# Recurrent scan with a transformer tile beside it: the output projection's halves, their filler and the widening change places

## Chip, cores and metric

One core of a Trainium2 chip. The metric is the device time of one execution in microseconds, lower is better. TensorE can be granted one of two clocks, 1.2 or 2.4 GHz.

## What is computed

Input x is (4, 16, 16, 64): four images of 256 positions with 64 channels, float32. Three layers follow, each added to what it gets:

```
x = x + deformable_conv(group_norm(x))         # 3x3, bilinear samples
t = tokens(x)                                  # (4, 256, 64)
t = t + attention_block(layer_norm(t))         # 8 heads of 32
t = t + scan(layer_norm(t))                    # 256 steps in order
```

The attention block, with y its projected output:

```
y  = o @ w_out.T + b_out
x1 = layernorm(y + x)
ff = (gelu(y @ w1.T) * (y @ wv.T)) @ w2.T
return layernorm(ff + x1)
```

The scan, one step per token and all four images at once (the forget gate is computed by the reference, but enters nothing):

```
i, o = sigmoid(xi_t + h @ V_i), sigmoid(xo_t + h @ V_o)
g = tanh(xg_t + h @ V_c)
c_new = h * c + i * g
h_new = o * tanh(c_new)
```

## The kernel before, in words

The 256 tokens are cut in NT = 8 tiles of TT = 32 tokens (32 x 4 images = 128 rows). A **prologue** does the convolution, the keys and values of all tokens and the attention of tile 0. Then come the 256 steps of the scan, in one loop over g that every engine has in its own program (EVERY, from -14 to 259; steps of the scan are 0 to 255). The attention of tile m is done beside the scan steps of tile m - 1, in pieces that are hung on steps by hand: `at(g)` gives, for each tile at work in step g, its own count o = g - (32 m - 32), from -9 to 31; where the text says step 18 of a window, o is 18. For tile 0 the steps from o = 18 on have a negative g: nothing of the scan runs beside them and they are the last part of the prologue.

**A step of the scan.** TensorE adds h @ V to the gates in PSUM (`gate_sums`, L727, 12 matmuls, waits for the H of the step before); ScalarE takes tanh of two gates (L896), then of the third (L900); VectorE scans the cell (L1232), ScalarE takes its tanh (L903), VectorE writes H (L1242) and at once the next step's SU (L1226). TensorE's order within a step is gate sums, then filler (`fill`, L396: matmuls on zeros into an idle bank that nobody reads, in pieces of up to 512 columns), then the tile's pieces (`beside`). VectorE has its pieces ahead of the cell's scan (`beside_gates`) or behind it (`beside_tanh`); ScalarE has them at the end of the step.

**How much filler.** `planned(g)` adds fixed prices (ns) of the pieces in a step; what is left of NS_STEP = 780 is filled at NS_FILL = 54 ns per 128 columns, at most 1536 columns. In the prologue's steps (g below 0) filler is 512 or 1536 columns by another rule, none at o = 19 and 20.

**The pieces around the change.** The heads' result O comes in two halves (`heads_out`, VectorE L1110, at o = 11 and 19; both at o = 18 for tile 0). The last weighing of a tile (`weigh`, L568) is at o = 18. O is projected twice: `project_turned` (L628, 128 x 64 array shape) gives y with channels on partitions, in b_t; `project` (L637, 128 x 128) gives y with tokens on partitions, in b_et. Each has a half per half of O. AY (ScalarE L914, end of step 19) waits for both turned halves. `widen` (L649) multiplies AY by the two wide matrices, part 0 at o = 20 and part 1 at o = 21; GE (ScalarE L889, end of step 20) waits for part 0. VectorE has R1 = y + residual at o = 21 (L1154, waits for both plain halves), its statistics (L1114) behind the scan of the same step, its aggregate (L1118) at o = 22, for tile 0 ahead of the gated product (L1160, o = 22, waits for GE), then FF (L1169, o = 23). `narrow` (L655) is at o = 24 and waits for FF; then R2, the layer norms, `turn_input` (L661, o = 30) and `preload` (L680, o = 31), which the first step of the scan waits for.

Of the kernel before, what the change touches and what calls it, by code (L numbers as in the profile page):

```python
# [54 lines left out]
EXP_SHIFT = 20.0  # L55
HEADS = (11, 19)
FIRST_TILE_FROM = 18
PROJECT = 18
SUMMED = 21
WIDEN = 20  # L60
# [21 lines left out]
COLS_EARLY = 512  # L82

NS_SCORES, NS_TURN, NS_WEIGH, NS_QUERIES = 570, 300, 320, 580
NS_PROJECT, NS_WIDEN, NS_NARROW, NS_INPUT, NS_PRELOAD, NS_STATES = 430, 545, 420, 140, 600, 210


K_ID, K_PAIR = 0, P
# [18 lines left out]
def hybrid_kernel(nc, x_fm2, x_fm, conv_w, dcn_w, attn_w, lstm_w, vecs, consts, out):  # L107
    ctx = ExitStack()
    with ctx:
# [139 lines left out]
        def start(m):  # L249

            return m * STEPS - LEAD

        def at(g):

            return [(m, g - start(m)) for m in range(NT) if (FIRST if m else FIRST_TILE_FROM) <= g - start(m) < LEAD]

        def leaving(g):

            m, o = divmod(g - OUT_LAG, STEPS)
            return m - 1 if o == 0 and 1 <= m <= NT else None  # L260
# [5 lines left out]
        TURN_AT = [2 * u + 2 for u in range(NU)]  # L266
# [3 lines left out]
        def queries_at(m):  # L270

            return -6 if m == 1 else -9
# [4 lines left out]

        EVERY = range(start(0) + FIRST_TILE_FROM, LAST + OUT_LAG + 2)

# [12 lines left out]
        def queries_ready(m, n):  # L292

            return B + NU * (m - 1) + n
# [96 lines left out]
        def _(pe):  # L391
            def fill(cols, idle):

                while cols >= 128:
                    n = min(cols, 512)
                    nc.tensor.matmul(idle[:, 0:n], FB[:, 0:P], FB[:, 0:n], start=True, stop=True)  # L396
                    cols -= n
# [116 lines left out]
            def queries(m):  # L514
                pe.wait_ge(et_sb, NU * m)
                pe.wait_ge(r_done, 2 * m - 1)
                for hg in range(HG):
                    mm = nc.tensor.matmul(b_et[:, P * hg:P * (hg + 1)], AW[0:C, AW_QKV + P * hg:AW_QKV + P * (hg + 1)],
                                          YF[0:C, :, TT * m:TT * (m + 1)], start=True, stop=True)
                mm.then_inc(q_mm, 1)  # L520
# [18 lines left out]
            def turn_probs(m, u):  # L539
                i = NU * m + u  # L540
                if m >= 1 and u == 0:
                    pe.wait_ge(q_done, queries_ready(m, NU))
                elif i >= 1:
                    pe.wait_ge(et_sb, i)
                if m == 0 and u >= NU - 2:
                    pe.wait_ge(e_first, u - (NU - 2) + 1)
                else:
                    pe.wait_ge(e_norm, i + 1 - (0 if m == 0 else 2))
                for h in range(HALVES):
                    mm = nc.tensor.transpose((b_et if m else b_et_first)[:, P * h:P * (h + 1)],  # L550
                                             E[:, i % 2, P * h:P * (h + 1)], ident)
                mm.then_inc(et_mm, 1)
# [68 lines left out]
            def project_turned(m, hg):  # L621

                pe.wait_ge(o_done, HG * m + hg + 1)
                if hg == 0 and m >= 1:
                    pe.wait_ge(xt_done, m)
                if hg == 0 and m >= 2:
                    pe.wait_ge(out_add, m - 1)
                mm = nc.tensor.matmul(b_t[0:C, 0:P], AW[:, AW_OUT + C * hg:AW_OUT + C * (hg + 1)],  # L628
                                      O[:, hg, :, :].rearrange("p t b -> p (t b)"), start=(hg == 0), stop=(hg == HG - 1),
                                      skip_group_check=True)  # L630
                if hg == HG - 1:
                    mm.then_inc(yf_mm, 1)

            def project(m, hg):

                pe.wait_ge(o_done, HG * m + hg + 1)
                mm = nc.tensor.matmul(b_et[:, 0:C], O[:, hg, :, :].rearrange("p t b -> p (t b)"),  # L637
                                      AW[:, AW_OUT + C * hg:AW_OUT + C * (hg + 1)], start=(hg == 0), stop=(hg == HG - 1),
                                      skip_group_check=True)
                if hg == HG - 1:  # L640
                    mm.then_inc(y_mm, 1)

            def widen(m, part):

                dst = (b_t, b_pv)[part]
                pe.wait_ge(ay_done, m + 1)
                for j in range(FT):
                    w = AW_W1 + P * (FT * part + j)
                    mm = nc.tensor.matmul(dst[:, P * j:P * (j + 1)], AW[:, w:w + P], AY[:], start=True, stop=True)  # L649
                mm.then_inc(h_mm, 1)  # L650

            def narrow(m):
                pe.wait_ge(ff_done, m + 1)
                for j in range(FT):
                    mm = nc.tensor.matmul(b_t[:, 0:C], FF[:, j, :], AW[:, AW_W2 + C * j:AW_W2 + C * (j + 1)],  # L655
                                          start=(j == 0), stop=(j == FT - 1))
                mm.then_inc(ff_mm, 1)

            def turn_input(m):
                pe.wait_ge(ln3_done, m + 1)  # L660
                nc.tensor.transpose(b_t[0:C, 0:P], LN3[:], ident).then_inc(xt_mm, 1)  # L661
# [8 lines left out]
            def preload(m):  # L670

                pe.wait_ge(xt_done, m + 1)
                if m >= 2:
                    pe.wait_ge(gates, STEPS * (m - 1))
                    pe.wait_ge(o_gate, STEPS * (m - 1))
                else:
                    pe.wait_ge(lw_done, 6)
                    pe.wait_ge(zeroed, 7)
                for gate in range(3):
                    nc.tensor.matmul(gate_out(m, gate, slice(0, C), slice(0, P)), UW[:, gate, :],  # L680
                                     XT[:, m, :, :].rearrange("p s b -> p (s b)"), start=(gate != 1), stop=True,
                                     skip_group_check=True)

            def planned(g):

                ns = 0
                for m, o in at(g):
                    ns += NS_QUERIES * (o == queries_at(m)) + NS_SCORES * (o in SCORES_AT) + NS_WEIGH * (o in WEIGH_AT)
                    ns += NS_TURN * (o in TURN_AT) + NS_PROJECT * (o in (PROJECT, PROJECT + 1)) + NS_PROJECT // 2 * (o == PROJECT + 2)
                    ns += NS_WIDEN * (o in (WIDEN, WIDEN + 1)) + NS_NARROW * (o == NARROW)  # L690
                    ns += NS_INPUT * (o == CELL_INPUT) + NS_PRELOAD * (o == CELL_READY)
                return ns + NS_STATES * (leaving(g) is not None)

            def beside(g):

                for m, o in at(g):
                    if o == CELL_INPUT:
                        turn_input(m)
                    if o == CELL_READY:
                        preload(m)  # L700
                    if o == queries_at(m):
                        queries(m)
                    if m > 0 and o in SCORES_AT:
                        scores(m, SCORES_AT.index(o))
                    if m > 0 and o in WEIGH_AT:
                        weigh(m, WEIGH_AT.index(o))
                    if m > 0 and o in TURN_AT:
                        turn_probs(m, TURN_AT.index(o))
                    if o == PROJECT:
                        project_turned(m, 0)  # L710
                        project(m, 0)
                    if o == PROJECT + 1:
                        project_turned(m, 1)
                    if o == PROJECT + 2:
                        project(m, 1)
                    if o == WIDEN:
                        widen(m, 0)
                    if o == WIDEN + 1:
                        widen(m, 1)
                    if o == NARROW:  # L720
                        narrow(m)
                if leaving(g) is not None:
                    turn_states(leaving(g))
# [8 lines left out]
            for g in EVERY:  # L732
                if 0 <= g < LAST:
                    m, s = divmod(g, STEPS)
# [9 lines left out]
                    fill(cols, idle)  # L744
                elif start(0) + PROJECT <= g < start(0) + CELL_READY and g not in (start(0) + PROJECT + 1, start(0) + PROJECT + 2):
                    fill(COLS_EARLY if g < start(0) + NARROWED else MOST, b_cell[1])
# [173 lines left out]
        def _(dve):  # L920
# [216 lines left out]
            def beside_gates(g):  # L1137

                for m, o in at(g):
                    if m == 0 and o == FIRST_TILE_FROM:  # L1140
                        heads_out(m, 0)
# [171 lines left out]
```

## Time and profile before

| | us |
|---|---|
| median of 3 runs | 392.46 (391.75 to 392.54) |
| the profiled execution | 390.11 |
| its span | 388.2 |
| TensorE, VectorE, ScalarE, GpSimd busy | 348.3, 239.2, 238.4, 62.3 |
| granted TensorE clock, mean share of full | 0.999 |

How to read it: the span runs from the first instruction to the last of one execution; the device time has some 1.9 us around it. TensorE's busy time is made high by filler, and says little on what bounds the kernel. L numbers are lines of the kernel. A timeline row gives start, duration (of the whole group where it says x2 or more), engine, line, operation, what it writes and reads, shape, count, and in brackets how long the engine was idle before it and who ended that.

### The profile page before, as it was taken

To read this page: it belongs to the slowest core of one execution; us is meant where nothing else is said; L and a number is where in the kernel's file an instruction comes from. 1 tells how busy PE (TensorE), PEld (TensorE's weight loads), DVE (VectorE), ACT (ScalarE), POOL (GpSimd) and SP (SyncE) were. 2 spreads that over 40 slices of the span, in tenths; PEclk is the share of its full clock that TensorE was granted. 3 is DMA by queue.
4 is the path that set the end of the run, shared out by engine and by line. 5 is a ranking of instruction groups with operands and counts; after the bars stand their busy time and mean duration, and the time that the engine had idled before them with its cause. 6 is when DMAs were issued, how large, how long until landed. Compare 5 with 4: busy or idle time off the path is not lost.

```text
span 388.2 us, 14584 instructions
## 1 busy us (share of the span) xinstructions
PE 348.3 (90%) x5457; PEld 203.0 (52%) x5509; DVE 239.2 (62%) x1225; ACT 238.4 (61%) x1125; POOL 62.3 (16%) x139
## 2 busy tenths in 40 slices
PE   7999997888999898999989988999899899988886
PEld 2576674554555555455645554555555455543332
DVE  2498763554757675666666666756665766564443
ACT  2586754625865786678567756865786578534443
POOL 3101100432102110212012102111110211110000
PEclk9999999999999999999999999999999999999999
DMA  8000000000000000000000000000000000000000
GB/s 261 4 2 10 10 12 14 15 2 3 3 3 3 5 3 4 3 5 5 2 3 8 2 3 2 8 2 3 6 4 3 3 6 2 5 2 6 2 3 4
DMA packets 4804, 4.29 MB, mean 11 GB/s; under 512 B 3837, under 2 KB 4286, under 8 KB 4734
## 3 DMA queue, kind: packets, MB, share of 16 engines
q1 hardware_dynamic: 4432, 2.84, 2.6%
q8 instruction: 43, 0.70, 0.8%
q10 hardware_dynamic: 302, 0.52, 0.4%
q14 instruction: 27, 0.22, 0.2%
HBM read 2.57 MB, written 0.26 MB: 7 GB/s over the span
## 4 chain that ended last, share of the span: by engine, by line
PE 40%; ACT 24%; DVE 23%; issue 11%; POOL 1%; DMA 1%; ACTq 0%; DVEq 0%
PE bank L727 15%; DVE bank L1232 10%; ACT E L824 9%; DVE H L1242 7%; ACT bank L896 7%; ACT bank L903 7%; PE bank L396 5%; PE bank L463 3%; PE bank L453 2%; PE bank L424 2%; PE bank L550 2%; PE bank L568 1%; PE bank L680 1%; DVE A L1059 1%; PE bank L637 1%
## 5 line engine op out<-in xcount | busy, mean ns | idle before, releaser
L396 PE MATMUL bank<-FB 128*128 128x512 bf16 (+3 forms) x445 | 129.2, 362 | 9.0 <-issue 7.8
L727 PEld LDWEIGHTS bank<-H,VW 64*32 64x32 f32 x3072 | 52.3, 106 | 108.7 <-DVE H L1242 107.2
L727 PE MATMUL bank<-H,VW 64*32 64x4 f32 x3072 | 74.6, 176 | 20.0 <-DVE H L1242 2.8
L896 ACT ACTIVATE bank<-bank 64x8 f32<-64x8 f32 x256 | 37.6, 147 | 75.7 <-PE bank L727 75.3
L1232 DVE TENSOR_TENSOR_SCAN bank<-bank,SU 64x12 f32<-64x12 f32 x256 | 48.5, 190 | 49.7 <-ACT bank L896 47.3
L1242 DVE SCALAR_TENSOR_TENSOR H<-TO,bank 64x4 f32<-64x4 f32 x256 | 40.8, 159 | 45.8 <-ACT bank L903 36.0
L373 POOL TENSOR_SCALAR E<-E,rinv 128x256 f32<-128x256 f32 x62 | 29.8, 481 | 130.7 <-DVE rinv L1042 130.6
L396 PEld LDWEIGHTS bank<-FB 128*128 128x128 bf16 x497 | 39.0, 98 | 21.1 <-issue 1.9
L903 ACT ACTIVATE bank<-bank 64x4 f32<-64x4 f32 x256 | 38.4, 150 | 16.0
L900 ACT ACTIVATE TO<-bank 64x4 f32<-64x4 f32 x256 | 43.7, 171 | 6.2
L1226 DVE SCALAR_TENSOR_TENSOR SU<-H,bank 64x4 f32<-64x4 f32 x256 | 41.3, 161 | 9.0
L536 PE MATMUL bank<-KF,QB 128*128 128x256 f32 x128 | 38.7, 384 | 0.7 <-DVE rinv L1042 0.7
L824 ACT ACTIVATE E<-bank,nmax 128x256 f32<-128x256 f32 x64 | 30.4, 475 | 3.8 <-DVE nmax L1034 2.3
L1027 DVE TENSOR_REDUCE nmax<-bank 128x1 f32<-128x256 f32 x64 | 27.1, 424 | 6.8 <-PE bank L536 4.8
L550 PE MATMUL bank<-K,E 128*128 128x128 f32 x128 | 27.4, 295 | 1.6 <-DVE E L1046 0.7
L832 ACT COPY ET<-bank 128x256 f32<-128x256 f32 x64 | 23.9, 374 | 4.6 <-PE bank L550 3.1
L536 PEld LDWEIGHTS bank<-KF,QB 128*128 128x128 f32 x128 | 22.7, 194 | 2.4 <-issue 2.0
L1059 DVE TENSOR_TENSOR A<-HAT 128x512 f32<-128x512 f32 x36 | 22.9, 681 | 0.1
L843 ACT COPY AT<-bank 128x512 f32<-128x512 f32 x36 | 19.1, 598 | 6.2 <-PE bank L453 6.2
L366 POOL TENSOR_SCALAR rs<-mv 128x1 f32<-128x1 f32 x24 | 5.4, 226 | 101.1 <-DVE mv L1118 101.1
L568 PE MATMUL bank<-ET,V 128*32 128x32 f32 x1024 | 21.2, 201 | 0.0
L453 PE MATMUL bank<-K,A 128*128 128x128 f32 x144 | 18.3, 277 | 0.0
(115 smaller groups left out, 344.3 us busy)
## 6 DMA issues: line engine op xcount, KB each, us to landing
AW<-in_attn_w SPq DMA_DIRECT2D x1, 768.5 KB, 8.0
DW<-in_dcn_w SPq DMA_DIRECT2D x1, 576.0 KB, 6.5
X<-in_x_fm SPq DMA_DIRECT2D x1, 256.0 KB, 3.2
X<-in_x_fm ACTq DMA_DIRECT2D x1, 256.0 KB, 5.2
T<-T0T SPq DMA_DIRECT2D x16, 16.0 KB, 1.8
Y<-YT SPq DMA_DIRECT2D x16, 16.0 KB, 1.8
out_dram<-OUT SPq DMA_DIRECT2D x8, 32.0 KB, 1.4
CW<-in_conv_w SPq DMA_DIRECT2D x1, 243.5 KB, 3.7
```

Source lines behind the costliest of these rows:

```text
L373: nc.gpsimd.tensor_scalar(E[:, i % 2, :], E[:, i % 2, :], rinv[:, i % 2:i % 2 + 1], 1.0, ALU.mult, ALU.mult).then_inc(e_norm, 1)
L396: nc.tensor.matmul(idle[:, 0:n], FB[:, 0:P], FB[:, 0:n], start=True, stop=True)
L536: nc.tensor.matmul(score_bank(m, u)[:, 0:N], QB[:, hg, b, :, :].rearrange("p h t -> p (h t)"), KF[:, hg, b, :], start=True, stop=True).the ...
L550: mm = nc.tensor.transpose((b_et if m else b_et_first)[:, P * h:P * (h + 1)], E[:, i % 2, P * h:P * (h + 1)], ident)
L727: mm = nc.tensor.matmul(gate_out(m, gate, r, slice(B * s, B * (s + 1))), VW[0:C, gate, r], H[0:C, (STEPS * m + s - 1) % RING, :], start=Fa ...
L824: nc.scalar.activation(E[:, i % 2, :], score_bank(m, u)[:, 0:N], ACT.Sigmoid, bias=nmax[:, i % 2:i % 2 + 1], accum_out=sum_of(m, u)).then_ ...
L896: nc.scalar.activation(GT[:, :, 1:3].rearrange("p b g -> p g b"), b_cell[m % 2][0:C, 0:2 * P].rearrange("p (g s b) -> p g s b", g=2, b=B)[ ...
L900: nc.scalar.activation(TO[:], gate_out(m, 2, slice(0, C), slice(B * s, B * (s + 1))), ACT.Tanh).then_inc(o_gate, 1)
L903: nc.scalar.activation(TC, CS[:, :, 2], ACT.Tanh, scale=0.5).then_inc(tanh_c, 1)
L1226: nc.vector.scalar_tensor_tensor(out=SU[:, :, 2], in0=H[0:C, (g - 1) % RING, :], scalar=0.5, in1=CS[:, :, 2], op0=ALU.mult, op1=ALU.mult). ...
L1232: nc.vector.tensor_tensor_scan(CS.rearrange("p b q -> p (b q)"), GT.rearrange("p b q -> p (b q)"), SU[:].rearrange("p b q -> p (b q)"), 0. ...
L1242: nc.vector.scalar_tensor_tensor(out=H[0:C, g % RING, :], in0=TO[:], scalar=1.0, in1=TC, op0=ALU.add, op1=ALU.mult).then_inc(h_done, 1)
```

## The change

Three edits, with the prices that go with them:

1. For tiles 1 to 7 the first half of `project_turned` goes from o = 18 to o = 17. Tile 0 keeps it at 18.
2. The step of its second half, o = 19, is priced at 780 ns (NS_LATE), so that no filler stands ahead of it. A half projection elsewhere is priced at 215 ns, and steps 17 and 18 get their filler by that: 1280 columns instead of 1536 in step 17, 512 instead of none in step 18, none instead of 768 in step 19.
3. In step 20 `widen` part 0 comes ahead of the second half of `project`, for all tiles.

```diff
+TURNED_HALF = 17
...
-NS_PROJECT, NS_WIDEN, NS_NARROW, NS_INPUT, NS_PRELOAD, NS_STATES = 430, 545, 420, 140, 600, 210
+NS_PROJECT, NS_LATE, NS_WIDEN, NS_NARROW, NS_INPUT, NS_PRELOAD, NS_STATES = 215, 780, 545, 420, 140, 600, 210
...
-                    ns += NS_TURN * (o in TURN_AT) + NS_PROJECT * (o in (PROJECT, PROJECT + 1)) + NS_PROJECT // 2 * (o == PROJECT + 2)
+                    ns += NS_TURN * (o in TURN_AT) + NS_PROJECT * (o in (TURNED_HALF, PROJECT, WIDEN)) + NS_LATE * (o == PROJECT + 1)
...
+                    if o == (TURNED_HALF if m else PROJECT):
+                        project_turned(m, 0)
                     if o == PROJECT:
-                        project_turned(m, 0)
                         project(m, 0)
                     if o == PROJECT + 1:
                         project_turned(m, 1)
-                    if o == PROJECT + 2:
-                        project(m, 1)
                     if o == WIDEN:
                         widen(m, 0)
+                        project(m, 1)
                     if o == WIDEN + 1:
                         widen(m, 1)
```

## Rows read from the trace of the kernel before

**Rows 1.** The page: the granted clock in 40 slices, the chain by engine

```profile
PEclk9999999999999999999999999999999999999999
...
PE 40%; ACT 24%; DVE 23%; issue 11%; POOL 1%; DMA 1%; ACTq 0%; DVEq 0%
```

**Rows 2.** One line's instructions (first row), then its timeline, steps 17 to 21

```profile
L1242 DVE SCALAR_TENSOR_TENSOR H<-TO,bank x256: 159/159/161, 92.8 to 385.6; 64x4 f32<-64x4 f32 x128
...
185.78 0.16 DVE L1242 SCALAR_TENSOR_TENSOR H<-TO,bank 64x4 f32<-64x4 f32 x1 [0.22 <-ACT bank L903]
...
186.92 0.16 DVE L1242 SCALAR_TENSOR_TENSOR H<-TO,bank 64x4 f32<-64x4 f32 x1 [0.22 <-ACT bank L903]
...
188.13 0.16 DVE L1242 SCALAR_TENSOR_TENSOR H<-TO,bank 64x4 f32<-64x4 f32 x1 [0.22 <-ACT bank L903]
...
189.30 0.16 DVE L1242 SCALAR_TENSOR_TENSOR H<-TO,bank 64x4 f32<-64x4 f32 x1 [0.22 <-ACT bank L903]
...
190.54 0.16 DVE L1242 SCALAR_TENSOR_TENSOR H<-TO,bank 64x4 f32<-64x4 f32 x1
```

**Rows 3.** Timeline, TensorE, steps 17 to 19 of tile 3's window

```profile
185.09 0.82 PE L396 MATMUL bank<-FB 128*128 128x512 bf16 x3
...
186.00 0.29 PE L727 MATMUL bank<-H,VW 64*32 64x4 f32 x12
...
186.48 0.43 PE L628 MATMUL bank<-O,AW 128*64 128x128 f32 x2
...
186.84 0.43 PE L637 MATMUL bank<-AW,O 128*128 128x64 f32 x2
...
187.21 0.29 PE L727 MATMUL bank<-H,VW 64*32 64x4 f32 x12
```

**Rows 4.** Timeline, TensorE: filler followed by another array shape, prologue and step 16

```profile
80.03 0.38 PE L396 MATMUL bank<-FB 128*128 128x512 bf16 x1
...
80.34 0.33 PE L568 MATMUL bank<-ET,V 128*32 128x32 f32 x16
...
183.95 0.28 PE L396 MATMUL bank<-FB 128*128 128x256 bf16 x1
...
184.16 0.33 PE L568 MATMUL bank<-ET,V 128*32 128x32 f32 x16
```

**Rows 5.** Timeline, all engines, steps 19 to 21 of the same window

```profile
187.31 0.39 DVE L1110 COPY O<-bank 128x128 f32<-128x128 f32 x1
...
187.66 0.27 PE L396 MATMUL bank<-FB 128*128 128x256 bf16 x1 [0.16 <-issue]
...
187.86 0.43 PE L628 MATMUL bank<-O,AW 128*64 128x128 f32 x2
...
188.33 0.36 ACT L914 ACTIVATE AY<-bank,AW 64x128 f32<-64x128 f32 x1 [0.23 <-PE bank L628]
...
188.72 0.15 ACT L896 ACTIVATE bank<-bank 64x8 f32<-64x8 f32 x1
...
189.54 0.39 ACT L889 ACTIVATE GE<-bank 128x256 f32<-128x256 f32 x1 [0.27 <-PE bank L649]
...
189.95 0.15 ACT L896 ACTIVATE bank<-bank 64x8 f32<-64x8 f32 x1
```

**Rows 6.** Timeline, all engines, the prologue's projections of tile 0

```profile
83.33 0.22 DVE L1154 TENSOR_TENSOR R<-bank,YB 128x64 f32<-128x64 f32 x1 [1.18 <-PE bank L637]
83.44 0.52 PEld L649 LDWEIGHTS bank<-AY,AW 128*128 128x128 f32 x4 [0.28 <-ACT AY L914]
...
83.85 0.18 DVE L1118 BATCH_NORM_AGGREGATE mv<-st 128x2 f32<-128x6 f32 x1
...
83.99 0.38 PE L396 MATMUL bank<-FB 128*128 128x512 bf16 x1
...
84.19 0.38 ACT L889 ACTIVATE GE<-bank 128x256 f32<-128x256 f32 x1 [0.80 <-PE bank L649]
...
84.60 0.42 DVE L1160 SCALAR_TENSOR_TENSOR GE<-GE,bank 128x256 f32<-128x256 f32 x1 [0.57 <-ACT GE L889]
```

## The prediction

> **What bounds the kernel now.** I read the page first. The chain of waits that ended last is shared by TensorE 40%, ScalarE 24%, VectorE 23% and issue 11% [rows 1]: no engine is the bound, a loop through all of them is. The line's own view shows which: 256 writes of H (L1242), from 92.8 to 385.6 us, that is 1.148 us each on average [rows 2]. The last one is followed only by the way out, so time can be won or lost in two places: the 92.8 us ahead of the first step, and steps that are longer than the plain one. A plain step is the 1.14 us from the H at 185.78 to that at 186.92 [rows 2], which is step 18 of the window in which tile 3 is made ready. The next three take 1.21, 1.17 and 1.24 us [rows 2]. These are steps 19, 20 and 21, and they are where the change works: 0.07 + 0.03 + 0.10 = 0.20 us over plain. Seven windows have them (tiles 1 to 7), so 1.4 us in all, 0.36% of the time, is the most that the steady part can give.
>
> The timeline tells why each is long. In step 18 TensorE has gate sums at 186.00, then weigh, L628 at 186.48, L637 at 186.84, and comes to the next gate sums (L727) only at 187.21 [rows 3], where H's end (186.92 + 0.16) would have let it start at 187.14: the usual lag is 0.06, as from 185.94 to 186.00 [rows 2, 3]. So step 18 is overfull and step 19 is 0.07 late. In step 20 the AY evacuation (188.33 to 188.69) holds ScalarE, whose gate tanh starts at 188.72, 0.03 late. In step 21 it is GE (189.54 to 189.93) ahead of the tanh at 189.95, 0.10 late [rows 5].
>
> **Part by part, steady steps.** First what a move on TensorE costs. Between fillers the pitch is 0.22 us for 512 columns (three starts and an end make 0.82 with 0.39 for the last [rows 3]). A 512-column filler followed by another array shape takes 0.31 (80.03 to 80.34) and one of 256 columns 0.21 (183.95 to 184.16) [rows 4]: both are 0.1 over their columns. L628 followed by L637 takes 0.36, L637 followed by L727 0.37 [rows 3]. The schedule in the code prices a half projection at 215 ns. The Trainium skill, "TensorEngine Tiling (Array Packing)", Key Properties, says that changing the tiling mode drains the TensorE; the rows agree with 0.1 us a change. By that rule the moved half brings step 17 one change more; without it the case is the second rival below.
>
> Step 17 now: filler 1280 columns (3 matmuls, at 185.09, 185.31, 185.52) in place of 1536, then L628. The last filler has 256 columns, so L628 starts 0.21 later at 185.73 [rows 4] and the next gate sums can start 0.36 later, at 186.09, where they stand at 186.00 now [rows 3]. **Step 18 starts 0.09 late**, a new cost. The fillers have no wait and cannot shrink.
>
> Step 18: gate sums to gate sums took 1.21. L628 goes (0.36); but the planned cost falls to 535 of 780, so a 512-column filler comes in ahead of weigh (0.32). 1.21 - 0.36 + 0.32 = 1.17: **0.03 late instead of 0.07**. The later weigh (by 0.32, ends near 186.9) is still ahead of the O copy at 187.31 that waits for it [rows 5].
>
> Step 19: the two fillers (768 columns) go and L628 waits for the O copy alone. That ends at 187.70; with the lag of 0.06 L628 starts at 187.76 rather than 187.86 [rows 5]. The gate sums of step 20 are queued behind this wait, but not due before 188.31, when L628 has been through for 0.2 us. AY moves 0.10 up to 188.23, and the tanh could follow 0.39 later at 188.62 (188.33 to 188.72 [rows 5]); it is due at 188.65. **Step 20 is plain**, 0.03 gained.
>
> Step 20: widening starts 0.06 behind AY's end (188.59), at 188.65. L637 comes 0.55 behind it, at 189.20 (L649 at 83.44 to the next matmul at 83.99 [rows 6]). From L637 to the gate sums it is 0.37 in row 3 with its weight load exposed; behind the widening this load can hide. The lower end is 0.27, as if the 0.1 of the change of shape were free; I take the middle, 0.32, so 189.52. H of step 20 comes at 189.23 (186.92 + 1.17 + 1.14) and its gate sums are due at 189.45: **step 21 is 0.07 late, instead of 0.10**. ScalarE is no longer what delays it: GE starts 0.75 behind the widening (83.44 to 84.19 [rows 6]) at 189.40, the tanh could follow 0.41 later at 189.81 [rows 5], and is due at 189.86. The late y reaches R1 when that is due anyway.
>
> Sum per window: after 0.09 + 0.03 + 0 + 0.07 = 0.19, before 0.20. Times seven: -0.07 us. No DMA, SP or POOL instruction moves.
>
> **Part by part, the prologue.** Tile 0 keeps step 18 for its first half, so only the swap touches it: L637 stood in the time in which TensorE waited for AY, and now comes behind L649. The widening (83.44) and GE (84.19) stay. L637 would start at 83.99 and y be ready near 84.37, so R1, at 83.33 before, starts at 84.41: 1.08 later. VectorE works in program order: R1, statistics, aggregate (L1118 at 83.85, so 0.52 behind R1), then the gated product L1160, which stood at 84.60, held by GE alone [rows 6]. Now the aggregate runs at 84.93 to 85.11 and L1160 starts at 85.14: **0.54 later**. VectorE's idle 0.57 us ahead of L1160 was the cover for R1; it is used up. The narrow projection (L655) waits for the product, and behind it stand only fillers and chained steps up to the first gate sums, so all 0.54 reaches the first H. The second widening is pushed by 0.25 as well, and ends before L1160 does. The Trainium skill, "TensorE: Matmul & The Clock Gate", Part 1, has VectorE as a strict FIFO; the order of these rows agrees.
>
> **Sum.** -0.07 + 0.54 = +0.47 us. The profiled execution took 390.11 (span 388.2 and 1.9 around it) and would take 390.6. The three runs have a median of 392.46, 2.3 us above it; I carry the difference over: **392.9 us**. About 0.2% (0.8 us) is what a measurement of this kernel can tell from no change; the shown runs differ by as much.
>
> **Rivals.** (a) *Removing filler gains nothing in step 19, and the plain projection is in the way (slower).* L628 started 0.16 behind the O copy's end; if that lag, not the filler, set it, AY stays at 188.33 and the tanh at 188.72, now 0.07 late. The widening is at 188.75, L637 at 189.30, and with the exposed load's 0.37 the gate sums of step 21 at 189.67, due at 189.52: 0.15 late. A window then costs 0.09 + 0.03 + 0.07 + 0.15 = 0.34, 0.14 more than before: 7 x 0.14 + 0.54 = +1.5 us, 394.0. It decides from about 0.05 us per window. Against it: the 0.21 of rows 4 explains 187.66 (the last filler [rows 5]) to 187.86 wholly, and H to L727 shows 0.06. Chance 0.15.
> (b) *The fillers overlap what follows (faster).* If L628 and weigh cost their 215 and 320 ns as planned, steps 17 to 20 fit and all of the 0.20 goes: -1.4 + 0.54 = -0.9 us, 391.6. Against it: rows 3 show 0.36. Chance 0.08.
> (c) *The prologue doesn't feel the late y*, because R1's group does not stand ahead of the product on the chain: then -0.1 us, 392.4. For it: VectorE idles 0.57 us there. Against it: the program order. Chance 0.12.
> (d) *The clock falls* from 2.4 to 1.2 GHz, since 512 filler columns of each window go and step 19 gets an idle 0.4 us. It is granted in full in all 40 slices [rows 1], and the idle of a plain step does not disturb it now. If the gate sums of three steps per window ran at half rate (about 0.2 us each), it would cost 4 us. Chance 0.03.
>
> **How the numbers follow.** My forecast has 0.62. Its own range is 392.5 to 393.4 (per window +-0.04 from 0.27 or 0.37 and the lag, so +-0.3, with the spread of medians), of which about 0.07 lies above +0.2%. Same: 0.55 + 0.12 (c) = 0.67. Slower: 0.07 + 0.15 + 0.03 = 0.25. Faster: 0.08. The range reaches down towards (b) and up into (a): 391.9 to 394.0.
>
> **What would show it.** Steps 18, 19, 20, 21 of a window at 1.23, 1.17, 1.14 and 1.21 us; L628 of step 17 0.21 behind a 256-column filler; L628 of step 19 at 0.06 behind the O copy; L1160 of the prologue about 0.54 later with no idle ahead of it, and the first H at 93.35. Step 18 at 1.14 would refute my price of step 17; a first H at 92.8 the prologue's; step 21 above 1.27 would speak for (a); a clock below full for (d).

## The result: 404.0 us, 3% slower, because TensorE's clock falls

The changed kernel takes 404.03 us (median of 6 runs, 403.08 to 412.41) beside 391.54 us for the kernel before (6 runs, 389.96 to 392.54): ratio 1.032, interval 1.0281 to 1.0359. The forecast was 392.9, with 391.9 to 394.0.

A ratio here leaves out a kernel's runs that are more than 1.5% above its fastest, and since these are often the very runs in which the clock fell, the median over all runs and the mean clock granted stand beside it. The forecast stood on the first three runs of the kernel before (median 392.46); with six the median is 391.54, 0.9 us lower, which is small beside the miss.

The profiled execution took 406.87 us, its span 405.1 instead of 388.2. The page of the changed kernel: span, busy time, granted clock in 40 slices, chain by engine and by line, and the filler's group; the last row is the chain by line of the kernel before.

```profile
span 405.1 us, 14622 instructions
PE 373.9 (92%) x5502; PEld 212.6 (52%) x5502; DVE 239.8 (59%) x1225; ACT 238.4 (59%) x1125; POOL 62.1 (15%) x139
...
PEclk9999999999999995799999959995899999889999
...
PE 49%; ACT 20%; DVE 20%; issue 9%; POOL 1%; DMA 1%; ACTq 0%; DVEq 0%
PE bank L728 14%; PE bank L397 13%; ACT E L825 9%; DVE bank L1233 9%; ACT bank L897 5%; DVE H L1243 5%; ACT bank L904 5%; PE bank L464 3%; PE bank L650 2%; PE bank L454 2%; PE bank L425 2%; PE bank L551 2%; PE bank L519 1%; PE bank L569 1%; PE bank L681 1%
...
L397 PE MATMUL bank<-FB 128*128 128x512 bf16 (+3 forms) x490 | 151.6, 392 | 1.2 <-DVE FB L927 1.2
...
PE bank L727 15%; DVE bank L1232 10%; ACT E L824 9%; DVE H L1242 7%; ACT bank L896 7%; ACT bank L903 7%; PE bank L396 5%; PE bank L463 3%; PE bank L453 2%; PE bank L424 2%; PE bank L550 2%; PE bank L568 1%; PE bank L680 1%; DVE A L1059 1%; PE bank L637 1%
```

The clock row was full in all 40 slices [rows 1]; now it has four dents, one in each of the windows of tiles 2, 4, 5 and 7. ScalarE and VectorE are busy as long as before (238.4 and 239.8 us, 238.4 and 239.2 before), and the filler (L397, line numbers are one higher from here on) is in the chain with 13% instead of 5%. TensorE is 26 us longer by the two pages, but that is too much: the trace of the kernel before lacks some of the filler's matmuls (L396 has 445 matmuls and 497 weight loads, L397 in the changed kernel 490 and 490). At some 0.2 us each the 52 make about 10 us, an estimate, so some 16 us are left, about what the span grew by (16.9).

Where does it fall? The windows view over steps 19, 20 and 21 of tile 2's window, then over the low stretch and what follows it (columns: stretch, length, busy time of each engine with its instructions, granted clock, DMA share, GB/s):

```profile
150.83:152.00 1.17, 0.88 (x16) 0.57 (x16) 0.89 (x4) 0.47 (x3) 0.00 (x0) 1.00 0.00 0
152.00:153.14 1.14, 0.98 (x16) 0.80 (x16) 0.51 (x4) 0.83 (x4) 0.00 (x0) 0.77 0.05 14
153.14:154.98 1.84, 1.84 (x20) 1.62 (x20) 0.84 (x6) 0.85 (x4) 0.00 (x0) 0.50 0.00 0
...
152.62:166.28 13.66, 13.66 (x124) 7.72 (x127) 6.66 (x36) 5.13 (x29) 1.57 (x4) 0.50 0.01 3
```

The clock is full (1.00, 2.4 GHz) up to the middle of step 20, then 0.50 (1.2 GHz) for 13.7 us, in which this view shows TensorE never idle. All four falls begin in step 20 of their window, at 152.62, 231.13, 272.09 and 350.59 us; the first three last 13.7 us, the fourth 6.8. In step 19 TensorE had been busy for 0.88 of 1.17 us. Steps 19 and 20 of the kernel before, in tile 3's window, were busier:

```profile
186.92:188.13 1.21, 1.05 (x17) 0.73 (x18) 0.90 (x4) 0.47 (x3) 0.00 (x0) 1.00 0.00 0
188.13:189.30 1.17, 1.12 (x20) 0.94 (x18) 0.51 (x3) 0.83 (x4) 0.00 (x0) 1.00 0.00 0
...
187.43 0.11 PEld L396 LDWEIGHTS bank<-FB 128*128 128x128 bf16 x2
```

Of the two fillers in step 19, whose weight loads are the last row, only the second has its matmul in the trace (187.66, [rows 5]); so 1.05 of 1.21 is too little. r6 below has the same filler in step 19 and a complete trace, and shows it busy throughout:

```profile
189.40:190.61 1.21, 1.21 (x18) 0.72 (x18) 0.90 (x5) 0.47 (x3) 0.00 (x0) 1.00 0.00 0
```

But the busy time of one step doesn't say where the clock falls. Step 19 of tile 3's window in the changed kernel is as thin, and the clock held there, as it did in the windows of tiles 1 and 6:

```profile
192.27:193.43 1.16, 0.87 (x16) 0.57 (x16) 0.88 (x4) 0.47 (x3) 0.00 (x0) 1.00 0.00 0
```

At half clock most steps take 1.71 us instead of 1.14 (1.6 to 1.9 where other pieces stand in them), and what fills them is the filler with the pieces behind it. From the changed kernel's timeline, the H of the long step 21, the three fillers of step 22 and its H:

```profile
154.98 0.16 DVE L1243 SCALAR_TENSOR_TENSOR H<-TO,bank 64x4 f32<-64x4 f32 x1
...
155.98 1.46 PE L397 MATMUL bank<-FB 128*128 128x512 bf16 x3
...
156.68 0.16 DVE L1243 SCALAR_TENSOR_TENSOR H<-TO,bank 64x4 f32<-64x4 f32 x1 [0.16 <-ACT bank L904]
```

Three such matmuls took 0.82 us in [rows 3], and the next gate sums are queued behind them. The loss adds up: first H of three windows in a row, those of tiles 2, 3 and 4,

```profile
130.18 0.16 DVE L1243 SCALAR_TENSOR_TENSOR H<-TO,bank 64x4 f32<-64x4 f32 x1
...
171.70 0.16 DVE L1243 SCALAR_TENSOR_TENSOR H<-TO,bank 64x4 f32<-64x4 f32 x1
...
208.27 0.16 DVE L1243 SCALAR_TENSOR_TENSOR H<-TO,bank 64x4 f32<-64x4 f32 x1
```

so tile 2's window takes 41.52 us with a fall and tile 3's 36.57 without one. The last H is at 402.45, against 385.58. Of these 16.87 us, 0.44 come before the first H, 16.6 in the four windows with a fall (4.8, 4.7, 4.8 and 2.3), and the other windows give back 0.1.

**Where the clock held, the steps are what was forecast.** The timeline of tile 3's window, steps 17 to 21, answers to [rows 2, 3, 5]:

```profile
190.34 0.71 PE L397 MATMUL bank<-FB 128*128 128x512 bf16 x3
...
190.98 0.43 PE L629 MATMUL bank<-O,AW 128*64 128x128 f32 x2
...
191.34 0.29 PE L728 MATMUL bank<-H,VW 64*32 64x4 f32 x12
...
192.27 0.16 DVE L1243 SCALAR_TENSOR_TENSOR H<-TO,bank 64x4 f32<-64x4 f32 x1 [0.22 <-ACT bank L904]
...
192.65 0.38 DVE L1111 COPY O<-bank 128x128 f32<-128x128 f32 x1
...
193.09 0.43 PE L629 MATMUL bank<-O,AW 128*64 128x128 f32 x2 [0.29 <-DVE O L1111]
...
193.43 0.16 DVE L1243 SCALAR_TENSOR_TENSOR H<-TO,bank 64x4 f32<-64x4 f32 x1 [0.21 <-ACT bank L904]
...
194.52 0.33 PE L638 MATMUL bank<-AW,O 128*128 128x64 f32 x2
194.57 0.16 DVE L1243 SCALAR_TENSOR_TENSOR H<-TO,bank 64x4 f32<-64x4 f32 x1 [0.22 <-ACT bank L904]
...
194.79 0.29 PE L728 MATMUL bank<-H,VW 64*32 64x4 f32 x12
...
195.72 0.16 DVE L1243 SCALAR_TENSOR_TENSOR H<-TO,bank 64x4 f32<-64x4 f32 x1
```

Steps 18 to 21 take 1.24, 1.16, 1.14 and 1.15 us. L629 in step 19 starts 0.06 behind the O copy's end (193.03), the gate sums (L728) at 191.34 0.36 behind L629, and those at 194.79 0.27 behind L638. Two windows are not like the other five, before as after: tile 1's step 20 takes 1.40 us before and 1.35 now, and tile 4's step 18 takes 1.35 before and 1.46 now, with step 19 plain. The prediction read one window and took it times seven.

### The profile page after: what moved, and what is told of

Read it like the earlier page. It is cut to its first block, busy times and chain, and to the rows that moved or that the text cites. A ratio compares the mean times of both kernels' runs of the same rounds, so it can differ in the third digit from the quotient of the medians.

```text
span 405.1 us, 14622 instructions
## 1 busy us (share of the span) xinstructions
PE 373.9 (92%) x5502; PEld 212.6 (52%) x5502; DVE 239.8 (59%) x1225; ACT 238.4 (59%) x1125; POOL 62.1 (15%) x139
## 4 chain that ended last, share of the span: by engine, by line
PE 49%; ACT 20%; DVE 20%; issue 9%; POOL 1%; DMA 1%; ACTq 0%; DVEq 0%
PE bank L728 14%; PE bank L397 13%; ACT E L825 9%; DVE bank L1233 9%; ACT bank L897 5%; DVE H L1243 5%; ACT bank L904 5%; PE bank L464 3%; PE bank L650 2%; PE bank L454 2%; PE bank L425 2%; PE bank L551 2%; PE bank L519 1%; PE bank L569 1%; PE bank L681 1%
## 5 line engine op out<-in xcount | busy, mean ns | idle before, releaser
L397 PE MATMUL bank<-FB 128*128 128x512 bf16 (+3 forms) x490 | 151.6, 392 | 1.2 <-DVE FB L927 1.2
L728 PEld LDWEIGHTS bank<-H,VW 64*32 64x32 f32 x3072 | 54.6, 110 | 108.2 <-DVE H L1243 104.5
L728 PE MATMUL bank<-H,VW 64*32 64x4 f32 x3072 | 77.0, 178 | 17.1 <-DVE H L1243 1.2
L1243 DVE SCALAR_TENSOR_TENSOR H<-TO,bank 64x4 f32<-64x4 f32 x256 | 40.8, 159 | 46.0 <-ACT bank L904 36.5
L397 PEld LDWEIGHTS bank<-FB 128*128 128x128 bf16 x490 | 40.2, 101 | 23.4 <-issue 6.0
L904 ACT ACTIVATE bank<-bank 64x4 f32<-64x4 f32 x256 | 38.4, 150 | 15.8
L569 PEld LDWEIGHTS bank<-ET,V 128*32 128x32 f32 x1024 | 14.1, 110 | 9.2 <-issue 3.3
```

The lines of the kernel that those rows point to most:

```text
L569: mm = nc.tensor.matmul((b_pv if m else b_pv_first)[r, P * hg + TT * b:P * hg + TT * (b + 1)], V[:, b, half, c], ET[:, i % 2, half, TT * h ...
L728: mm = nc.tensor.matmul(gate_out(m, gate, r, slice(B * s, B * (s + 1))), VW[0:C, gate, r], H[0:C, (STEPS * m + s - 1) % RING, :], start=Fa ...
L904: nc.scalar.activation(TC, CS[:, :, 2], ACT.Tanh, scale=0.5).then_inc(tanh_c, 1)
L1243: nc.vector.scalar_tensor_tensor(out=H[0:C, g % RING, :], in0=TO[:], scalar=1.0, in1=TC, op0=ALU.add, op1=ALU.mult).then_inc(h_done, 1)
```

## Experiments

All steps below are those of the windows of tiles 1 to 7, and where one number stands for a step it is that of the five like windows; the clock is the mean share granted over an execution, and "full" stands for 0.99 or more. Of the 71 executions of the kernel before that stand beside these runs, 66 have 0.995 or more and five 0.991 to 0.993. The profiled executions of r4, r6, r7 and r11 show a dip of 3.4 us in the prologue, at 70 to 71 us, where all these kernels are still the same; it is a likely cause of such values before, too, but no trace of the kernel before has one. "Full" doesn't exclude a single short fall in the steps: r11's profiled execution has that dip, one fall in the steps, and 0.991.

| run | filler columns in 17, 18, 19 | order of pieces | median, all runs (before) | runs with full clock |
|---|---|---|---|---|
| before | 1536, 0, 768 | old | 391.1 to 391.7 | all |
| changed | 1280, 512, 0 | new | 404.03 (391.54) | 0 of 6 |
| r1 | 1280, 512, 768 | new | 391.05 (391.69) | 12 of 12 |
| r2 | 1536, 0, 0 | old | 400.02 (391.69) | 0 of 4 |
| r3 | 0, 0, 768 | old | 419.45 (391.69) | 0 of 4 |
| r4 | 1536, 0, 768 | widening first | 392.20 (391.69) | 11 of 12 |
| r5 | 1536, 768, 0 | old | 399.60 (391.13) | 0 of 4 |
| r6 | 1024, 0, 768 | old | 395.82 (391.13) | 1 of 10 |
| r7 | 1280, 512, 512 | new, tile 0 old | 391.16 (391.13) | 9 of 12 |
| r8 | 1024, 384, 512 | new, tile 0 old | 389.73 (391.13) | 12 of 12 |
| r9 | 1280, 512, 0 | old | 398.47 (391.60) | 0 of 4 |
| r10 | 1536, 0, 768 | new | 396.77 (391.60) | 5 of 10 |
| r11 | 1024, 384, 256 | new, tile 0 old | 394.67 (391.60) | 1 of 10 |

### r1: the filler of step 19 back in the changed kernel

```diff
-                    ... + NS_LATE * (o == PROJECT + 1)
+                    ... + 430 * (o == PROJECT + 1)
```

> The changed kernel, but with 768 filler columns ahead of the second turned half in step 19, as in the kernel before. Theory A (the clock falls because step 19 has no filler): clock full in all slices, steps 18 to 21 at about 1.23, 1.17, 1.17 and 1.17 us, first H at 93.25, time within 0.5 us of the kernel before (391.5 to 392.5 beside its 391.5). Theory B (the clock falls because of the order in step 20, widening first, which leaves TensorE waiting for AY with nothing to do): the clock still falls, 400 us or more. Theory C (what counts is the number of filler columns in the window's steps 17 to 20 together): 2560 columns against 2304 before, so full clock, as in A.

391.05 us (390.85 to 392.41), ratio 1.0001 (0.9983 to 1.0019). Full clock in every run; steps 18 to 21 at 1.23, 1.17, 1.17, 1.19. With these 768 columns back, and all other edits in place, the 12.5 us are gone. Theory B, that the order in step 20 alone brings the fall, is refuted.

### r2: only this filler taken from the kernel before

```diff
                     cols = min(P * ((NS_STEP - planned(g)) // NS_FILL), MOST)
+                    if any(m and o == PROJECT + 1 for m, o in at(g)):
+                        cols = 0
```

> The kernel before, its only edit no filler in step 19 of the seven windows (768 columns less each). Theory A: the clock falls in some of the windows as in the changed kernel, 398 to 408 us. Theory B: the order in step 20 is the old one, so the clock holds and the time is about 391.3 (AY 0.1 us earlier, step 20 plain: -0.2 us in all). Theory C: 1536 columns against 2304, so it falls as in A.

400.02 us, ratio 1.0229 (1.0184 to 1.0275). The profiled execution falls four times again, in the windows of tiles 3, 4, 6 and 7, each time in step 20, for 3.4, 13.7, 3.4 and 3.4 us. The granted clock by slices shows the first, the second and the fourth; its last digit is the end of the program:

```profile
PEclk9999999999999999999899958999999999899998
```

So taking filler out of step 19 is enough for a fall. But it is not the only place:

### r3: the filler of step 17 taken instead

```diff
                     cols = min(P * ((NS_STEP - planned(g)) // NS_FILL), MOST)
+                    if any(m and o == PROJECT - 1 for m, o in at(g)):
+                        cols = 0
```

> The kernel before, its only edit no filler in step 17 of the seven windows (1536 columns less each, twice what step 19 loses), while step 19 keeps its 768. Theory A: the clock holds, 391.5 us. Theory C (the total of the window): 768 columns against 2304, so the clock falls in more windows than in the changed kernel, 404 us or more. Theory B: the clock holds.

419.45 us, ratio 1.0713 (1.0679 to 1.0748): all seven windows fall, from step 18, 19 or 20 on.

```profile
PEclk9999999999958995899799759995998799689999
```

Theory A, that step 19's filler alone matters, is refuted too, though this edit takes twice as many columns. Nothing was added to any step, and every window has a fall, so I put all 28 us down to the clock.

### r4: the widening ahead of the projection, alone

```diff
-                    if o == PROJECT + 2:
-                        project(m, 1)
                     if o == WIDEN:
                         widen(m, 0)
+                    if o == PROJECT + 2:
+                        project(m, 1)
```

> The kernel before, its only edit the widening ahead of the plain projection in step 20, for all eight tiles. Theory A: the clock holds; the first H comes 0.45 us later (93.25), step 21 loses 0.03 to 0.09 of its excess in seven windows, together within 0.5 us of the kernel before. Theory B: the clock falls, 398 us or more.

392.20 us, ratio 1.0031 (1.0006 to 1.0056), no fall in the steps of its profiled execution; one run of 12 had 0.982. Step 21 goes from 1.24 to 1.18 or 1.19, and the first H comes 0.35 us later behind the first O copy of the prologue than before (11.83 against 11.48 us).

### r5 and r6: as many columns elsewhere, and fewer elsewhere

Theory C counts the filler columns of steps 17 to 20: 2304 before, 1792 in the changed kernel. r5 keeps 2304 with none in step 19; r6 has 1792 with step 19 untouched. Each kernel has one of the last two lines of this edit:

```diff
+                    for m_, o_ in at(g):
+                        cols = {18: 768, 19: 0}.get(o_, cols) if m_ else cols    # r5
+                        cols = {17: 1024}.get(o_, cols) if m_ else cols          # r6
```

> The kernel before with the 768 filler columns of step 19 moved to step 18 (none in 19); steps 17 to 20 keep their 2304. Theory C (the columns of these steps together decide): the clock holds; step 19 starts some 0.4 us late in seven windows, so about 394.5 us. Theory A in its softer form (the columns next to the idle of steps 19 and 20 decide): the clock falls in some windows and the time is 400 us or more.

> The kernel before with 1024 filler columns in step 17 instead of 1536, and 768 in step 19 as before: 1792 columns in steps 17 to 20, as many as the changed kernel has. Theory C: the clock falls as in the changed kernel, 398 to 408 us. Theory A, softer form: step 19 has its filler, so the clock holds, 391.7 us.

r5: 399.60 us, ratio 1.0232 (1.0192 to 1.0271), clock 0.967 to 0.980 in its four runs. Step 19 is 1.64 us, 0.43 longer than before in six windows and 0.29 in one, which is 2.9 us; the other 5 to 6 are the clock, which falls in four windows of the profiled execution. r6: 395.82 us over all runs (390.12 to 398.99), ratio 1.0074 (1.0041 to 1.0107). The profiled execution falls in two windows; one of its ten runs has a full clock (0.998), and the time of the kernel before. A total that is kept doesn't save r5, so theory C is refuted, and a step 19 that is kept doesn't save r6 (nor r3). Both the amount and the place count.

### r9 and r10: the change taken apart

r9 has the changed kernel's filler and the old order, r10 the new order and the old filler; the edit shows the line of each.

```diff
+                        cols = {17: 1280, 18: 512, 19: 0}.get(o_, cols) if m_ else cols      # r9, on before
+                        cols = {17: 1536, 18: 0, 19: 768}.get(o_, cols) if m_ else cols      # r10, on changed
```

> The kernel before with the changed kernel's filler alone: 1280, 512 and 0 columns in steps 17, 18 and 19; the projections and the widening stay where they were. Theory D (the clock falls where array work gets thin over steps 17 to 20, whatever the order of the pieces): it falls in several windows, 398 us or more; step 18 keeps 1.14 and step 19 becomes some 0.3 us late. Theory E (the moved half and the widening ahead of the projection are needed for the fall): clock full, about 393.7 us from the late step 19.

> The changed kernel with the filler of the kernel before: 1536, 0 and 768 columns in steps 17, 18 and 19; the moved half and the widening first stay. Theory D: clock full; step 18 at 1.34 (0.2 late: 256 columns more ahead of L628 than in the changed kernel), step 19 plain, 20 at 1.17, 21 at 1.19; about 0.7 us above the kernel before with the prologue's 0.4. Theory E: the clock falls, 398 us or more.

r9: 398.47 us (395.40 to 406.07), ratio 1.0114 (1.0070 to 1.0158), all four runs below full clock. Its late step 19 (1.53 us) explains 2.1 us of it. r10: five of ten runs are at 391.07 to 393.72 with full clock, ratio 1.0032 (1.0000 to 1.0064), five at 399.8 to 405.8 with 0.947 to 0.970. So the filler alone brings falls in every run, as theory D expected (thin array work over steps 17 to 20, whatever the order), but the order alone brings them in half of its runs, which D did not expect. The moved half leaves step 18 with one projection instead of two, and r10 puts nothing in its place; r1, with 512 columns there, held in all twelve runs. That this is the reason is argued: no run moves the half alone, and as the profiled execution of r10 is one that held, no trace shows where its clock falls.

### r7, r8 and r11: a version that keeps the clock

All three are the changed kernel with tile 0 in the old order and other columns in steps 17, 18, 19.

```diff
+                    if o == WIDEN and m == 0:
+                        project(m, 1)
                     if o == WIDEN:
                         widen(m, 0)
+                    if o == WIDEN and m > 0:
                         project(m, 1)
...
+                        cols = {17: 1280, 18: 512, 19: 512}.get(o_, cols) if m_ else cols    # r7
+                        cols = {17: 1024, 18: 384, 19: 512}.get(o_, cols) if m_ else cols    # r8
+                        cols = {17: 1024, 18: 384, 19: 256}.get(o_, cols) if m_ else cols    # r11
```

> The changed kernel with 512 filler columns back in step 19 (1280, 512, 512: the 2304 of the kernel before) and, for tile 0 alone, the plain projection ahead of the widening as before. 512 columns end before the O copy does, so L628 should start as early as with none. If the filler's loss is the whole cause of the slowdown, the clock holds; steps 18 to 21 at 1.23, 1.17, 1.14 and 1.15 us; the first H back at 92.8; 0.4 to 0.6 us below the kernel before, 391.2. If the shape of the work still lets the clock fall, 396 us or more.

> As the run with 512 columns in step 19, but with 1024 in step 17 and 384 in step 18, so that L628 and L638 no longer make steps 18 and 19 late: steps 18 to 21 at 1.14, 1.14, 1.14 and 1.15 us. It has 1920 columns in all. If the clock holds, 1.2 to 1.4 us below the kernel before (390.3); by theory C it lies between the 1792 that fell and the 2304 that held, so it may fall in some windows: then 394 us or more.

> The fitted version (1024, 384, 512) with 256 columns instead of 512 in step 19. No step is longer for it, so with a full clock it would be as fast (0.3% below the kernel before). Theory D: it is thinner than everything that held (1664 columns), so the clock falls in some windows, 393 us or more.

r7: 391.16 us, ratio 1.0001 (0.9976 to 1.0027); its profiled execution fell once in the steps, in tile 4's window, for 13.7 us, and three of twelve runs had 0.978, this one among them. r8: **389.73 us (388.98 to 391.46), ratio 0.9967 (0.9949 to 0.9985)**, faster than both kernels, 0.994 or more in all twelve runs. r11: 394.67 us over all runs, ratio 1.0070 (1.0031 to 1.0110). It has 256 columns less in step 19, 0.1 us of TensorE's time per window; nine runs of ten are below 0.99, and the tenth falls once in the steps all the same. From the timeline of r8, tile 3's window (H, the copy and L909 are those of L1243, L1111 and L904 above):

```profile
185.58 0.16 DVE L1248 SCALAR_TENSOR_TENSOR H<-TO,bank 64x4 f32<-64x4 f32 x1 [0.22 <-ACT bank L909]
186.72 0.16 DVE L1248 SCALAR_TENSOR_TENSOR H<-TO,bank 64x4 f32<-64x4 f32 x1 [0.22 <-ACT bank L909]
...
187.10 0.38 DVE L1116 COPY O<-bank 128x128 f32<-128x128 f32 x1
187.15 0.39 PE L397 MATMUL bank<-FB 128*128 128x512 bf16 x1
...
187.54 0.43 PE L629 MATMUL bank<-O,AW 128*64 128x128 f32 x2
...
187.85 0.16 DVE L1248 SCALAR_TENSOR_TENSOR H<-TO,bank 64x4 f32<-64x4 f32 x1 [0.22 <-ACT bank L909]
...
188.99 0.16 DVE L1248 SCALAR_TENSOR_TENSOR H<-TO,bank 64x4 f32<-64x4 f32 x1 [0.22 <-ACT bank L909]
...
190.17 0.16 DVE L1248 SCALAR_TENSOR_TENSOR H<-TO,bank 64x4 f32<-64x4 f32 x1
```

Steps 18 to 20 are plain (1.14, 1.13, 1.14); step 21 is 1.18 where 1.15 was expected. The 512 columns of step 19 run while O is being copied: L629 starts at 187.54, 0.06 behind the copy's end, just as with no filler. From first to last H it takes 291.77 us against 292.77 before, 0.14 us per window.

## Why the prediction was wrong

**The step that failed is rival (d).** I gave the fall of the clock 0.03, with the argument that "the idle of a plain step does not disturb it". That took one full clock row [rows 1] as proof of a margin, and the forecast's sum has no term for the clock. The row says that the schedule before was enough in that execution, not by how much. In its place the runs show four falls of the clock and 16.6 us for them. And they show how little there was to spare: 512 columns less than before in one step of 32 (r6), or 256 less than r8 (r11), put nine runs of ten below 0.99. The Trainium skill, "TensorE: Matmul & The Clock Gate", Part 1, says that the gate follows how busy the engine has recently been and knows a half and a full rate. The traces agree on the rates: their stretches are at 1.00 or 0.50. On the first the runs agree in kind, since taking filler away brings the falls, but a step's busy time doesn't tell a window that falls from one that holds (0.88 of 1.17 us and 0.87 of 1.16).

**Its price was mis-sized as well.** I had three steps per window at 0.2 us each, 4 us in all, on the notion that only the gate sums would be slower. The rows show 0.57 us for most steps (1.71 against 1.14), since fillers and pieces laid out for the full clock then take longer than the step: eight steps in each of three falls and four in the last, 16.6 us.

**Step 17's price: right.** L629 starts 0.21 behind the last filler and holds the gate sums back, so step 18 takes 1.23 or 1.24 us where 1.23 was forecast; r8, with 256 columns less there, has 1.14. **Step 18's price: right**, step 19 takes 1.16 or 1.17 for 1.17. **Step 19's: right**, the lag is 0.06 and step 20 is plain. Rival (a) is refuted with this. Rival (b), fillers that overlap what follows, is refuted by step 18's 1.23.

**Step 20's term: at the lower end of its bound.** I took 0.32 us from L637 to the gate sums out of 0.27 to 0.37; it is 0.27 (194.52 to 194.79), and may be less there, as these gate sums start just 0.06 behind the end of H, when they are due. So step 21 is 1.15 and not 1.21.

**The prologue: right in kind, 0.35 instead of 0.54 us.** The changed kernel's timeline:

```profile
84.45 0.23 DVE L1155 TENSOR_TENSOR R<-bank,YB 128x64 f32<-128x64 f32 x1 [2.21 <-PE bank L638]
...
84.97 0.18 DVE L1119 BATCH_NORM_AGGREGATE mv<-st 128x2 f32<-128x6 f32 x1
85.07 0.39 DVE L1161 SCALAR_TENSOR_TENSOR GE<-GE,bank 128x256 f32<-128x256 f32 x1
...
85.49 0.42 DVE L1170 TENSOR_TENSOR FF<-bank,GE 128x256 f32<-128x256 f32 x1
```

R1 came 1.03 later behind the O copies than before and used up the idle time ahead of the product, as said. But L1161 starts 0.10 behind the start of the aggregate, not 0.21, and before the aggregate has ended: it doesn't wait for it. That is 0.11 of the 0.19 missing; R1 itself gives 0.05, and the product, 0.39 us long instead of 0.42, the rest. The 0.44 in the first H are this 0.35 and 0.09 by which the whole prologue ran later. Rival (c) is refuted; r8, with tile 0 in the old order, is back at 11.48 us from the O copy to the first H.

Without the clock the sum would have been 7 x (0.09 + 0.03 + 0 + 0.01 - 0.20) + 0.35 = -0.1 us. No run shows just this. The windows of the changed kernel that hold come near it (tiles 3 and 6: 0.07 and 0.09 us less than before, tile 1: as long), and r1, whose steps 20 and 21 are 0.03 and 0.04 longer, is level with the kernel before within 0.2%.

**What stays open.** Why r7 (1280, 512, 512) fell in three runs of twelve and r8 (1024, 384, 512) in none, though r8 has less filler; twelve runs each may not tell them apart. Which executions fall: r10 has the same program at 391.1 and at 405.8 us. Which windows fall within one, as tiles 1, 3 and 6 held in the changed kernel's. And how long a fall lasts. No run here varied what differs between executions. Besides, r1 to r4 ran on one chip, r5 to r8 on a second and r9 to r11 on a third: each is measured beside the kernel before on its own chip, but r11 against r8, or r10 against r1, compares two chips, and no kernel but the one before was run on several of them.

## What to carry to other kernels

Where matmuls on nothing keep a clock up, they are part of the schedule's contract: a change that removes some, or that leaves a step with less real work, must say what keeps the clock, and a full clock row is no evidence of a margin. Put such filler where TensorE waits anyway (512 columns beside the O copy cost nothing here), and cut it only where it delays something. Look at every run's granted clock, not at the profile's alone: r10 and r7 have executions in which the clock holds, and others 1.6 to 3.8% above their own fastest.

## What the hardware showed beyond expectation

A clock that fell could stay low although TensorE was busy without a break: 13.66 us of 13.66 in the low stretch above. It doesn't always: r6's two falls in the steps and r5's four lasted 3.4 us each, with TensorE busy throughout as well. The falls came in or just behind the steps that had lost work (steps 18 to 21 in every profiled execution with one), but most of their cost lies in the steps behind, where the work is as before. And at 2.4 GHz a filler followed by a piece in another array shape takes 0.1 us more than the filler's columns, in the four places looked at: 0.31 and 0.32 us for 512 columns (80.03 to 80.34 before, 191.56 to 191.88 in the changed kernel) and 0.21 for 256, twice. A piece in the filler's own shape follows 512 columns by 0.23 (195.01 to 195.24). The plan in the code, at 54 ns per 128 columns and nothing for the change, prices step 17 at 755 ns of 780 when it overruns its step by 0.09 us.
